# A chain of graph layers on one core: layer-norm roots by a power on GpSimd, beta added to the residual in pass 5, ScalarE applying the gated pass's second norm

## What is computed

```python
def _layernorm(x, axis=-1, eps=1e-05):
    m = jnp.mean(x, axis=axis, keepdims=True)
    v = jnp.var(x, axis=axis, keepdims=True)
    return (x - m) / jnp.sqrt(v + eps)

# L0: relu(adj @ (f1 * (adj @ (x @ W1)))), then adj @ (f2 * (adj @ (h1 @ W2)))
# L1: concat(x, adj @ x) @ weight
# L2: messages = x @ W_msg + b_msg; q, k = messages @ W_q, messages @ W_k
#     gates = sigmoid(q @ k.T / scale + gate_bias) * adj * recency_prior   (recency_prior is adj)
#     updated = relu(concat(x, gates @ messages) @ W_upd + b_upd)
#     out = (updated - mu) * rsqrt(var + LN_EPS) * ln_gamma + ln_beta
# L3: x1 = swish((adj @ x) @ W + b); x2 = swish((adj @ x1) @ W + b)
x = _layernorm(x + _L0_gnn_ref(x, adj, adj, ...))
x = _layernorm(x + _L1_gnn_ref(x, adj, ...))
x = _layernorm(x + _L2_gnn_ref(x, adj, adj, ...))
x = _layernorm(x + _L3_gnn_ref(x, adj, ...))
```

## Time and profile before

| | us |
|---|---|
| median of 3 runs | 1704.26 |
| lowest, highest | 1702.74, 1706.06 |
| the profiled execution | 1702.63 |
| its span in the profile | 1700.8 |
| TensorE busy | 1624.1 |
| VectorE busy | 1277.8 |
| ScalarE busy | 1099.7 |
| GpSimd busy | 11.3 |

### The profile page before, as it was taken

The page is one execution under the profiler, slowest core; times in us unless marked ns, Lnnn a source line. Parts: engine busy times, 40 slices in busy tenths (PEclk is TensorE's granted clock), DMA queues, the critical chain, the costliest instruction groups (busy, mean ns, idle before and its releaser), DMA issues. The chain is left out here.

```text
span 1700.8 us, 19344 instructions
## 1 busy us (share of the span) xinstructions
PE 1624.1 (95%) x7618; PEld 766.1 (45%) x7618; DVE 1277.8 (75%) x1423; ACT 1099.7 (65%) x757; POOL 11.3 (1%) x25
## 2 busy tenths in 40 slices
PE   7999999999999999999999999899998899999986
PEld 4444444444444444444454444343444344444432
DVE  6876537653766398738996998989899996455997
ACT  5766747774786586656666677676767666444653
POOL 2000000000000000000000000000000000000000
PEclk9999999999999999999999999999999999999999
DMA  9979789977999779977777354454545797665893
GB/s 356 412 296 403 289 366 396 371 287 332 370 392 426 293 299 413 374 298 297 272 277 292 125 218 162 164 198 153 194 174 199 296 380 281 253 236 190 344 343 124
DMA packets 68427, 490.79 MB, mean 289 GB/s; under 512 B 7824, under 2 KB 7984, under 8 KB 9328
## 3 DMA queue, kind: packets, MB, share of 16 engines
q1 hardware_dynamic: 67104, 485.00, 74.1%
q0 software_dynamic: 1088, 4.49, 0.8%
q10 hardware_dynamic: 144, 0.07, 0.0%
HBM read 420.32 MB, written 69.21 MB: 288 GB/s over the span
## 5 line engine op out<-in xcount | busy, mean ns | idle before, releaser
L932 DVE SCALAR_TENSOR_TENSOR a_lo<-a_ring,a_hi 128x2048 f16<-128x2048 f32 x332 | 750.2, 2287 | 289.8 <-ACT a_hi L735 285.6
L735 ACT ACTIVATE a_hi<-a_ring 128x2048 f16<-128x2048 f32 x332 | 627.7, 1905 | 298.1 <-PE spare L542 150.9
L542 PE MATMUL acc<-a_hi,y_hi 128*128 128x512 f16 x1584 | 477.0, 382 | 2.9 <-ACT a_hi L735 2.9
L542 PE MATMUL acc<-a_hi,y_lo 128*128 128x512 f16 x1584 | 476.1, 382 | 0.0
L554 PE MATMUL acc<-a_lo,y_hi 128*128 128x512 f16 x1584 | 420.0, 381 | 26.8 <-DVE a_lo L941 14.0
L554 PEld LDWEIGHTS acc<-a_lo,y_hi 128*128 128x128 f16 x1584 | 153.5, 98 | 222.2 <-DVE a_lo L941 20.5
L542 PEld LDWEIGHTS acc<-a_hi,y_lo 128*128 128x128 f16 x1584 | 155.9, 98 | 190.4 <-issue 5.9
L542 PEld LDWEIGHTS acc<-a_hi,y_hi 128*128 128x128 f16 x1584 | 155.9, 99 | 189.8 <-issue 12.0
L954 DVE SCALAR_TENSOR_TENSOR gates<-gates,a_ring 128x1024 f32<-128x1024 f32 x128 | 155.8, 1217 | 28.1 <-ACT gates L765 27.9
L748 ACT ACTIVATE a_hi<-gates 128x1024 f16<-128x1024 f32 x128 | 134.8, 1053 | 64.6 <-DVE gates L954 64.4
L941 DVE TENSOR_TENSOR a_lo<-gates,a_hi 128x1024 f16<-128x1024 f32 x128 | 155.7, 1217 | 0.0
(11 more groups left out here) (98 smaller groups left out, 681.0 us busy)
## 6 DMA issues: line engine op xcount, KB each, us to landing
a_ring<-adj_dram SPq DMA_DIRECT2D x332, 1024.0 KB, 7.5
saved_squares<-squares SPq DMA_DIRECT2D x64, 1024.0 KB, 12.7
a_ring<-saved_squares SPq DMA_DIRECT2D x64, 1024.0 KB, 4.8
x_T<-xt_dram SPq DMA_DIRECT2D x4, 512.0 KB, 8.2
x_rows<-x_dram POOLq DMA_DIRECT2D x1, 2048.0 KB, 12.9
out_dram<-x_rows POOLq DMA_DIRECT2D x3, 512.0 KB, 3.4
out_dram<-x_rows SPq DMA_DIRECT2D x2, 256.0 KB, 2.1
w<-W_dram POOLq DMA_DIRECT2D x2, 64.0 KB, 5.6
```

The costliest lines, as they stand in the source:

```text
L542: mm = pe.matmul(sums[:, h * BANK:(h + 1) * BANK], blk(y[:, y_pass % 2, :], st.j0 + s), slot(a_hi, st)[:, s, h * BANK:(h + 1) * BANK], sta ...
L735: act.activation(slot(a_hi, st), loaded(st), ACT.Copy, scale=2.0 ** A_EXP).then_inc(s_ahi, 1)
L932: dve.scalar_tensor_tensor(out=slot(a_lo, st).rearrange("p s c -> p (s c)"), in0=loaded(st).rearrange("p s c -> p (s c)"), scalar=2.0 ** A ...
```

## The change

Newton's steps are gone from VectorE. `moments_of` now ends with variance + eps, and GpSimd raises these numbers to the power -0.5 (`root_of`, an operation of 8 numbers a partition with a tile of -0.5). VectorE's normalisation waits for the semaphore `s_root` of GpSimd. GpSimd has a table of stages of its own, and each root stands in its queue ahead of the store of the same chunk.

In the gated pass beta is no longer added by `normalise_affine`. In pass 5, once `x` has been transposed for the next operand, `add_beta` adds beta to `x_rows` (one operation a chunk, after `y_low`). The gated pass then multiplies by gamma without waiting for the root (`times_gamma`), and `affine_residual` forms (that) * root + (x + beta) in one operation a block, so that the residual sum is gone as an operation. The second norm is applied by ScalarE (`normalise_again`) as root * val + shift, with shift = -mean * root from one small operation of VectorE (`shift`). Steps of the stages have moved with it.

```diff
+            def normalise_again(blocks):
+                def go(p, k):
+                    act.wait_ge(s_shift, k + 1)
+                    for b in blocks:
+                        op = act.activation(x_chunk(p, k)[:, b, :], val[:, b, :], ACT.Identity,
+                                            bias=stats[:, 2, b:b + 1], scale=stats[:, 1, b:b + 1])
+                    if b == CB - 1:
+                        op.then_inc(s_ln, 1)
+                return go
...
-                6: {1: [evacuate], 6: [relu], 23: [y_high]},
+                6: {1: [evacuate], 6: [relu], 20: [normalise_again(range(HB))], 21: [normalise_again(range(HB, CB))],
+                    23: [y_high]},
...
-                LAST_GATED: {0: [evacuate], 3: [relu], 14: [y_high]},
+                LAST_GATED: {0: [evacuate], 3: [relu], 11: [normalise_again(range(CB))], 14: [y_high]},
...
-            def rstd_of(blocks, moments_done, n):
...
-                dve.wait_ge(s_moments, moments_done)
-                dve.tensor_scalar(var, moments[:, blocks[0]:blocks[-1] + 1, 1], LN_EPS, None,
+                dve.wait_ge(s_moments, before + len(blocks))
+                first, end = blocks[0], blocks[-1] + 1
+                dve.tensor_scalar(stats[:, 0, first:end], moments[:, first:end, 1], LN_EPS, None,
                                   ALU.add).then_inc(s_var, 1)
-                dve.wait_ge(s_var, n)
-                dve.tensor_scalar(as_int(r), as_int(var), -0.5, float(RSQRT_GUESS), ALU.mult,
-                                  ALU.add).then_inc(s_guess, 1)
-                dve.wait_ge(s_guess, n)
-                for step in range(NEWTON):
...
+            def add_beta(p, k):
+
+                dve.wait_ge(s_rows, nth("rows", p, k, 1))
+                dve.tensor_tensor(x_chunk(p, k), x_chunk(p, k), over_blocks(bet), ALU.add).then_inc(s_xb, 1)
+
+            def times_gamma(p, k):
+
                 for b in range(CB):
                     dve.scalar_tensor_tensor(out=xn[:, b, :], in0=val[:, b, :], scalar=moments[:, b, 0:1], in1=gam[:, :],
                                              op0=ALU.subtract, op1=ALU.mult).then_inc(s_scaled, 1)
+
+            def affine_residual(p, k):
+
+                dve.wait_ge(s_root, nth("root", p, k, 0))
+                dve.wait_ge(s_xb, k + 1)
                 for b in range(CB):
                     dve.wait_ge(s_scaled, CB * (nth("resid", p, k) - 1) + b + 1)
-                    op = dve.scalar_tensor_tensor(out=xn[:, b, :], in0=xn[:, b, :], scalar=stats[:, 1, b:b + 1],
-                                                  in1=bet[:, :], op0=ALU.mult, op1=ALU.add)
-                op.then_inc(s_ln, 1)
+                    op = dve.scalar_tensor_tensor(out=val[:, b, :], in0=xn[:, b, :], scalar=stats[:, 1, b:b + 1],
+                                                  in1=x_chunk(p, k)[:, b, :], op0=ALU.mult, op1=ALU.add)
+                op.then_inc(s_res, 1)
+
+            def shift(p, k):
+
+                dve.wait_ge(s_root, nth("root", p, k, 1))
+                dve.scalar_tensor_tensor(out=stats[:, 2, :], in0=moments[:, :, 0], scalar=-1.0, in1=stats[:, 1, :],
+                                         op0=ALU.mult, op1=ALU.mult).then_inc(s_shift, 1)
...
-                6: {5: [values], 8: [ln_moments(0, s_nl, "nonlin")], 10: [ln_rstd(0)], 12: [normalise_affine],
-                    15: [residual], 17: [ln_moments(1, s_res, "resid")], 20: [ln_rstd(1)], 21: [normalise(1)],
-                    23: [y_low]},
+                    7: [qk_low(0, kT_hi, kT_lo, K_EXP)], 8: [qk_low(1, qT_hi, qT_lo, Q_EXP)], 9: [y_low, add_beta]},
+                6: {5: [values], 8: [ln_moments(0, s_nl, "nonlin")], 10: [times_gamma], 13: [affine_residual],
+                    16: [ln_moments(1, s_res, "resid")], 19: [shift], 23: [y_low]},
...
+                LAST_GATED: {2: [values], 4: [ln_moments(0, s_nl, "nonlin")], 5: [times_gamma], 6: [affine_residual],
+                    8: [ln_moments(1, s_res, "resid")], 10: [shift], 14: [y_low]},
...
+            pool.memset(neg_half[:, :], -0.5).then_inc(s_exponent, 1)
+
+            def root_of(blocks, n):
+
+                first, end = blocks[0], blocks[-1] + 1
+                pool.wait_ge(s_var, n)
+                pool.tensor_tensor(stats[:, 1, first:end], stats[:, 0, first:end], neg_half[:, first:end],
+                                   ALU.pow).then_inc(s_root, 1)
...
+            stages = {4: {1: [root(0)]}, 5: {2: [root(0)]}, 6: {8: [root(0)], 16: [root(1)]}, 8: {5: [root(0)], 6: [store]},
+                      LAST_GATED: {4: [root(0)], 8: [root(1)]}}
```

More of the change, by code:

```diff
@@ L72 @@
     "resid": {6: 1, 8: 1},
-    "ln": {4: 1, 5: 1, 6: 2, 8: 1},
+    "root": {4: 1, 5: 1, 6: 2, 8: 1},
+    "ln": {4: 1, 5: 1, 6: 1, 8: 1},
     "msg": {5: 1},
@@ L282, in over_features @@
             return v.unsqueeze(2).to_broadcast([P, CB, F])
-        def normalised(p, k, run=0):
-            return xn[:, :, :] if p == GATED and run == 0 else x_chunk(p, k)
         def x_chunk(p, k):
@@ L397, in y_source @@
                 return flat(rows[:, :, :])
-            return flat(val[:, :, :]) if p in (1, 3) else flat(normalised(p, k, 1))
+            return flat(val[:, :, :]) if p in (1, 3) else flat(x_chunk(p, k))
         block = ctx.enter_context(nc.Block())
@@ L997, in _, with root, go @@
                                pattern=[[-1, P]], channel_multiplier=1).then_inc(s_id, 1)
+            pool.memset(neg_half[:, :], -0.5).then_inc(s_exponent, 1)
[4 more added lines that the diff above has]
+                                   ALU.pow).then_inc(s_root, 1)
+            def root(run):
+                def go(p, k):
+                    if p > GATED or (p == GATED and (run or k)):
+                        pool.wait_ge(s_ln, NC * (p - 4) + k if p == GATED else NC * 3)
+                    root_of(range(CB), nth("root", p, k, run))
+                return go
             def store(p, k):
@@ L1012, in _ @@
             pool.dma_start(x_rows[:, :, :], x).then_inc(s_x, 16)
+            pool.wait_ge(s_exponent, 1)
             epilogue(stages, at, THE_END)
+            for h in range(HALVES):
+                root_of(range(h * HB, (h + 1) * HB), last("root", h + 1))
 def kernel(**inputs):
```

64 lines of the change are left out of this document (15 added, 49 removed).

## The result

The changed kernel takes 1678.16 us (median of 4 runs, 1676.16 to 1679.06), the kernel before 1704.59 beside it (1702.74 to 1706.06): a ratio of 0.9853 with a 95% interval of 0.9841 to 0.9864. That is 26.4 us less, where 32.9 were forecast; 1678 lies in the range and is 6.8 us above the forecast. The profiled execution took 1678.3 us around a span of 1676.0.

The account below looks back on a forecast made before the run. TensorE, busy 1624.1 of 1700.8 us, was taken as the bound, waiting mostly on VectorE's low halves or queue. Terms 15.0 + 8.3 + 3.1 + 3.8 + 2.7 = 32.9 us gave 1671.4 us, range 1661 to 1694.

Parts of the forecast that it names:

- Gated pass: Three full chunks: VectorE has 6.8 us less work, TensorE waits 2.9 instead of losing 7.9 us; 15.0 us gained.
- The walk: Gated pass: VectorE's lateness followed step by step, 0.33 us regained a unit, giving 2.9 us of TensorE waiting a chunk.
- Start of pass 7: Last gated chunk's normalisation: 6.8 us of VectorE plus 1.5 of clock, 8.3 us gained; ScalarE's 2 us block costs nothing.
- Passes 4 and 5: VectorE wins 1.0 us a chunk; four places and 0.5 of clock, less 1.0 for beta: 3.1 us gained.
- The detour: Root by GpSimd: 0.3 us there, power 0.5, 0.2 back, 1.0 us in all; range 0.6 to 2.5.
- The four places: Passes 4 and 5: where TensorE waits for a low half, worth at most 1.0, 0.8, 0.8 and 1.0, so 3.6 us.
- Pass 8: A 2.26 us split covers the detour, so 2.0 us go each time; 3.8 us of TensorE's waits won.
- the blocked port: Rival: GpSimd and VectorE block each other, 4 us in the gated pass, pass 8's cover gone; 1678, chance 0.15.
- The end: Last two halves: the second wins 1.0 us, the first 1.7 under the swish; 2.7 us gained.
- About as long as Newton's steps: Rival: the power takes about as long as Newton's steps, a detour of 2.5 us; 1681, chance 0.18.
- The slower case: Rival: very long power exposed in passes 4, 5 and the end; slower from about 5 us, 1717 at 6; chance 0.12.
- Loop bound elsewhere: Rival: ScalarE or loads limit instead; half of 15.0 and 2 of 8.3 us are left; 1685, chance 0.08.

Follow-up runs that it names:

- norm_on_vectore: The changed kernel with the gated pass's second norm back on VectorE and no shift; roots, beta and fused residual stay: 1676.67 us, 0.985.
- power_twice: The changed kernel with each root's power computed twice on GpSimd, the first into a spare tile: 1698.67 us, 0.9975.
- last_norm_later: The changed kernel with ScalarE's norm of the last gated chunk at step 13 instead of 11, behind two more splits: 1675.03 us, 0.9841.
- after_again: The changed kernel, unedited, measured and profiled a second time: 1679.08 us, 0.9854.
- newton_in_4_5: The changed kernel with Newton's steps on VectorE in passes 4 and 5 and GpSimd's power everywhere else: 1681.62 us, 0.9866.
- p8_no_cover: The changed kernel with pass 8's normalisation right behind the variance, so no split runs beside the root: 1678.6 us, 0.9859.

## Why the prediction was right, and where it was not

The time lies in the range, and the largest term came true. Three of the other four terms rest on steps that failed.

**Gated pass: right, 15.0 us predicted and 15.0 measured.** TensorE waits 3.2 us in the chunk shown where 2.9 were forecast, its wait for `a_lo` is 0.8 us where about 1 was the sign, and the clock doesn't fall. That the totals agree so closely is in part luck. The walk has 1.7 us of waiting for low halves, where there are 0.8, and 1.2 us behind ScalarE, where there are 1.7 (0.99 and 0.72). Its last wait of 1.2 us forgets the four units between the shift and `y_lo`: by the walk's own 0.33 us a unit they give 1.3 us back, and nothing would be left of it. It came about by ScalarE itself, whose four operations take 1.65 us in a row and not 1. And norm_on_vectore, with the eight normalisations back on VectorE, takes 264.8 us: of the 6.8 us that VectorE loses in a chunk, the 2.05 for these were lost again behind ScalarE, but for 0.4 us in all three chunks. The power's 2.5 us was under the units between moments and use, as the step said, and power_twice confirms it.

**Start of pass 7: right in kind, 8.3 predicted, 4.5 measured.** The failing step is "I cost it nothing" for ScalarE's block, on the ground that ScalarE is ahead by its ring. It had been waiting 6.72 us for the shift, so it was not ahead, and the block was 3.19 us, not 2. The cover was missing, and last_norm_later puts its price at 3.0 us, of which 2.6 are waits. The waits of the kernel before in the same stretch, 1313 to 1380 us:

```profile
PE acc L554 <- DVE a_lo L932: 6.9, 4, 3.7
PE rows L452 <- ACT z_T L654: 1.1, 1, 1.1
```

They sum to 8.0 us, in after to 6.1 and in last_norm_later to 3.5. So of the 4.5 us only 1.9 are waiting and 2.6 are the clock (0.95 there before, 1.00 after); with the norm later it is 4.5 and 3.0. VectorE's 6.8 us didn't all reach TensorE even then, and the clock gave back all of its 3 us where I took half. That clock is not certain either: after_again has the same waits and 63.0 us, so that by the same working the clock gave back 0.9 us in that execution.

**Passes 4 and 5: the number was right and the reason wrong.** 3.1 us was predicted and 3.3 measured, of which 1.6 was the clock's fall at 798 us in that one execution of the kernel before. Without it 1.3 us are left. Two steps fail. The detour: I took 1.0 us, with a power of 0.5 near GpSimd's own operations. (The trace before has one more of these than the memset, an affine select of 128x128 at 0.28 us, so it wasn't quite without arithmetic; it would have pointed the same way.) The step counts it without the variance, and so counted it is 1.7 us (1.92 less 0.20), of which the power is 1.64; VectorE wins 0.3 us a chunk and not 1.0. The four places: power_twice and the idle times of newton_in_4_5 show that the detour counts in all eight chunks. Eight times 0.29 us is 2.3; less beta's 1.0 that is 1.3, which is what is left without the clock, while the step's own four places would have given 0.2. Beta's 1.0 us was about right (0.6 to 0.9).

**Pass 8: wrong, 3.8 predicted, 0.7 measured.** Two steps fail. "The detour is covered" falls to the blocked port, so that VectorE wins 0.5 us a root and not 2; TensorE's waits for low halves fell from 2.4 us to 1.7. And the 3.8 us of waits for z_T, of which I gave back 1.4, are 3.8 still: ahead of each z_T stands a split that VectorE starts for the block that is due, and no root.

```profile
1592.57 2.29 DVE L921 SCALAR_TENSOR_TENSOR a_lo<-a_ring,a_hi 128x2048 f16<-128x2048 f32 x1
1594.77 1.22 DVE L800 SCALAR_TENSOR_TENSOR z_T<-acc,gates 128x1024 f32<-128x1024 f32 x1
```

**The end: 2.7 predicted, 2.3 measured.** Right. The power of four columns takes 1.01 to 1.03 us where I took 0.5; the first half's is partly under the swish (0.51 us of waiting).

**The rivals.** The blocked port was named at 1678 and that is the time, but by half for its reason: pass 8 lost its cover, as it said, while VectorE in the gated pass lost nothing (its gate products take 1.22 us beside a power, under the 1.3 that was the sign), and the 4 us that it put there were by chance close to the 3.8 that the start of pass 7 missed. "About as long as Newton's steps" is true of the detour (1.92 against 2.21 us from the variance on) and wrong by its time of 1681, because it took 2.5. The slower case was put at a detour of about 5 us; power_twice, with 3.5, still ends 4 us under the kernel before. But 1.6 us more of detour cost 20.5 us, where the prediction's rule of nine times the detour gives about 14. By these two runs, an estimate, the kernel turns slower at 3.8 us already. "Loop bound elsewhere" is what happened at the start of pass 7, to its smaller part: it left 2 of the 8.3 us there, and 4.5 came. In the gated pass, where it left half of the 15.0, it didn't happen.

## What to carry to other kernels

A handful of numbers a partition sent to a slower engine comes back hardly sooner than nine tiny operations of the fast one would be done (1.92 and 2.21 us); it pays where the fast engine is behind and has other work meanwhile, and this kernel got 19.5 of its 24.8 us in the three gated chunks and at the start of pass 7. An operation of VectorE with two SBUF inputs is no cover for a small one of GpSimd that it is issued ahead of: count the power from the end of that operation. When work goes to an engine "with room", look at what it waits for just before: ScalarE was 65% busy, and one block of 3.2 us in the wrong place cost 3.0 us of the span.

## What the runs showed of the hardware

GpSimd's power on f32 takes 1.64 us for 128x8 and 1.02 us for 128x4: by these two, an estimate of 0.4 us fixed and 0.15 us a column. Beside VectorE operations with two SBUF inputs it takes 2.5 us (products of 1.22 us) and 3.55 (splits of 2.29 us). The first power of the program took 1.68 us, and VectorE waited 1.87 us for it where it waits 1.75 in pass 5, so the first call paid about 0.1 us extra; the 6 us that the Trainium skill states for a freshly loaded kernel ("GPSIMD Engine Reference", "Instruction dispatch") don't show. ScalarE's norm of 128x128 with scale and bias from a tile takes 0.48 us, and in a row one starts every 0.39 us. TensorE's clock, after an idle time of the same place in the program, stayed at 2.4 GHz behind a wait of 3.34 us (p8_no_cover) and fell to 1.2 behind one of 2.98 (before): the length of the one wait doesn't decide it, and what does is open.
